# Cross-attention and a quantized feed-forward block on one core: another opening, and SyncE's transposes in another order

## The reference, cut to what matters

```python
x = x + xattn(layernorm(x), ctx)            # x: 4 x 2048 x 512, ctx: 4 x 154 x 512
x = x + ffn(layernorm(x), w1, b1, w2, b2, gamma, beta)

# xattn: the mask lets query i see key j only where j % 2048 == i
#   row i <  154:  out = (ctx[i] @ Wv) @ Wout + bout      (softmax of one term)
#   row i >= 154:  nothing is unmasked, all keys weigh the same:
#                  out = (mean(ctx) @ Wv) @ Wout + bout   (one row for the batch)
# ffn: h = layernorm(x)*gamma + beta
#   qlinear(h, w, b): round h to 8 bits by a scale per row, round w to -1, 0, 1
#     by the mean of |w| over the whole matrix, multiply, scale back, add b
#   out = qlinear(gelu(qlinear(h, w1, b1)), w2, b2)       # hidden 2048
```

## Time and profile before

| | |
|---|---|
| median of 3 runs (lowest, highest) | 584.91 us (582.09, 586.11) |
| profiled execution | 585.01 us, its span 583.3 us |
| mean granted TensorE clock | 0.965 |
| PE, DVE, ACT, POOL busy | 90%, 78%, 73%, 68% |

### The profile page before, as it was taken

One profiled execution on the slowest core, in us unless ns is written; L12 is line 12 of the kernel. 1 busy time (PEld: TensorE's weight loads), 2 busy tenths in 40 slices (PEclk: granted clock), 3 DMA queues, 4 the chain that ended last, 5 costly groups with the idle time before them and its releaser, 6 DMA issues.

```text
span 583.3 us, 7986 instructions
## 1 busy us (share of the span) xinstructions
PE 526.4 (90%) x2368; PEld 225.3 (39%) x2414; DVE 457.8 (78%) x754; ACT 424.5 (73%) x413; POOL 397.3 (68%) x530
## 2 busy tenths in 40 slices
PE   6968641798799998999999999999999999999997
PEld 3423210343344443444444444444444444444443
DVE  1167785986689897798998989898899989896553
ACT  0264443885688886888888888888888888887762
POOL 0016839886577878688887878787878787874100
PEclk9989775998999998999999999999999999999999
DMA  9992122455655556345555655555555555443432
GB/s 332 380 387 100 24 72 58 94 134 140 170 132 131 132 131 132 88 120 132 132 132 130 133 130 132 130 132 130 132 128 134 128 132 118 96 94 91 97 76 90
DMA packets 136686, 78.56 MB, mean 135 GB/s; under 512 B 114008, under 2 KB 114008, under 8 KB 136644
## 3 DMA queue, kind: packets, MB, share of 16 engines
q1 hardware_dynamic: 132948, 70.50, 48.4%
q10 hardware_dynamic: 3696, 7.55, 3.5%
HBM read 33.77 MB, written 17.00 MB: 87 GB/s over the span
## 4 chain that ended last, share of the span: by engine, by line
PE 66%; DMA 8%; POOL 7%; issue 6%; DVE 6%; SPq 3%; ACTq 3%; ACT 1%; POOLq 0%; DVEq 0%
PE py L841 31%; PE p L823 31%; DMA xqT<-xq 5%; PE p L816 3%; DMA hqT<-ctxm_d 3%; POOL hx L334 2%; SPq L219 2%; POOL xr L319 2%; DVE xr L681 1%; ACTq L454 1%; DVE stat L631 1%; POOL xr L338 1%; DVE w2q L622 1%; SPq L182 1%; POOL rstd L326 1%
## 5 line engine op out<-in xcount | busy, mean ns | idle before, releaser
L823 PE MATMUL p<-w1q,xqT 128*128 128x512 bf16 x996 | 237.2, 390 | 2.9 <-issue 2.0
L841 PE MATMUL py<-w2q,hqT 128*128 128x512 bf16 x1006 | 230.0, 379 | 1.0
L499 ACT ACTIVATE hid<-p,xdeq 128x1024 f32<-128x1024 f32 x128 | 141.9, 1110 | 40.0 <-PE p L823 39.8
L506 ACT ACTIVATE hq<-hid,hscale 128x2048 int8<-128x2048 f32 x64 | 128.1, 2002 | 45.6 <-DVE hscale L666 45.6
L841 PEld LDWEIGHTS py<-w2q,hqT 128*128 128x128 bf16 x1024 | 100.2, 98 | 120.8
L823 PEld LDWEIGHTS p<-w1q,xqT 128*128 128x128 bf16 x1024 | 97.1, 100 | 127.4 <-issue 26.6
L319 POOL TENSOR_TENSOR xr<-xr,attn 128x512 f32<-128x512 f32 (+1 forms) x61 | 86.5, 1438 | 13.3 <-issue 13.3
L660 DVE TENSOR_REDUCE hmax<-hid 128x1 f32<-128x1025 f32 x64 | 78.1, 1221 | 22.0 <-ACT hid L499 21.1
L656 DVE TENSOR_REDUCE hid<-hid 128x1 f32<-128x1024 f32 x64 | 77.5, 1211 | 18.7 <-ACT hid L499 18.7
L338 POOL TENSOR_TENSOR xr<-xr,b_b 128x512 f32<-128x512 f32 x64 | 87.3, 1384 | 0.0
L334 POOL TENSOR_TENSOR hx<-hx,beta_b 128x512 f32<-128x512 f32 (+1 forms) x63 | 80.6, 1300 | 1.7 <-ACT hx L486 1.7
(11 more groups left out here) (76 smaller groups left out, 284.7 us busy)
## 6 DMA issues: line engine op xcount, KB each, us to landing
out<-xr SPq DMA_DIRECT2D x64, 256.0 KB, 2.3
xr<-x SPq DMA_DIRECT2D x61, 256.0 KB, 3.0
wout<-wout_d ACTq DMA_DIRECT2D x8, 256.0 KB, 11.1
hid<-wvT SPq DMA_DIRECT2D x8, 256.0 KB, 12.2
raw<-w1T ACTq DMA_DIRECT2D x4, 512.0 KB, 11.6
raw<-w1T SPq DMA_DIRECT2D x4, 512.0 KB, 12.7
wout<-w2T SPq DMA_DIRECT2D x4, 512.0 KB, 8.2
xr<-w2T SPq DMA_DIRECT2D x2, 512.0 KB, 15.2
```

Of the source, the lines that this page charges most:

```text
L499: nc.scalar.activation(hid[:, t % 2, h * HALF:(h + 1) * HALF], p1[:, h * HALF:(h + 1) * HALF], ACT.Gelu, scale=col(xdeq, t)).then_inc(gelu ...
L506: nc.scalar.activation(hq8[:, t % 2, :], hid[:, t % 2, 0:HID], ACT.Copy, scale=col(hscale, t))\
L823: mm = nc.tensor.matmul(p1[:, n * D:(n + 1) * D], xT[:, k, :], w1q[:, k, n * D:(n + 1) * D], start=False, stop=(k == KD - 1))
L841: mm = nc.tensor.matmul(py[:, t % 2, :], hqT[:, t % 2, c // 2, c % 2, :], w2q[:, c, :], start=(c == 0), stop=(c == 2 * NJ - 1))
```

## The change

It does four things.

1. **Mean row of batch 0 from its own products.** Before, the row came out of Wv·Wout. Now the mean context row is made on PE first (two matmuls with ones, 128 and 26 rows), copied to all partitions by DVE; eight elementwise products of it with the Wv chunks (POOL for chunks 1, 2, 4, 6, 7, DVE for 0, 3, 5) are summed along the row by ACT (`mean_sum`), the sums weigh the Wout chunks on DVE (`mean_weighted`), and one matmul with ones, put after the 15th product, adds over partitions. The pick matrix is gone. The 108 rows are made much later, behind the first half of the first layer of tile 3.
2. **w2 in w1's raw buffer.** An eighth of w2 goes to `raw1` when w1 has been rounded there, so w2's loads wait for that rounding, and x tiles keep their own slots.
3. **Orders of the opening rewritten** on all five queues: Wv and Wout first, w1 behind them on SP alone, contexts later; x loads 0 to 13 before the loop; tiles 0 to 3 written out by hand; the loop starts at s = 4.
4. **In the loop** SP transposes the GELU bytes of tile s-1, then (odd s) the x pair, and only then stores and loads; POOL takes 1/std after the scale columns and adds b2 four tiles later.

```diff
+        w2raw = [raw1[:, j % 4, j // 4 * HALF:(j // 4 + 1) * HALF].rearrange("p (e n) -> p e n", e=2) for j in range(8)]
...
             def load_w2(j):
+                sp.wait_ge(wround_dve[0], j // 4 + 1)
+                sp.wait_ge(wround_act[0], j // 4 + 1)
...
             load_wv(0)
+            sp.dma_start(ctx_rows, ctx_b0[0:P, :]).then_inc(ctx_b0_loaded, 16)
+            sp.dma_start(ctx_end, ctx_b0[P:KV, :]).then_inc(ctx_b0_loaded, 16)
...
+            for s in range(4, T + LAG + 2):
+                if live(s - 1):
+                    transpose_h(s - 1)
+                if s % 2 == 1:
+                    for t in (s + 1, s + 2):
+                        if live(t):
+                            transpose_x(t)
                 if live(s - LAG - 1):
                     t = s - LAG - 1
                     sp.wait_ge(y_ready, t + 1)
                     sp.dma_start(out[t * P:(t + 1) * P, :], xr[:, t % XS, :]).then_inc(y_stored[t % XS], 16)
-                if live(s - 1):
-                    transpose_h(s - 1)
...
+            def mean_product(m):            # POOL; DVE has the same
+                pool.wait_ge(chunk_loaded[m], 32)
+                pool.wait_ge(ctx_mean_copied, 1)
+                if m >= 3:
+                    pool.wait_ge(vmean_done, m - 2)
+                pool.tensor_tensor(product[m % 3], wv[:, m // 4, m % 4, :], ctx_mean, ALU.mult).then_inc(vprod_pool, 1)
...
+            def mean_sum(m):                # ACT
+                nc.scalar.activation(product[m % 3], product[m % 3], ACT.Copy, accum_out=vmean[:, m:m + 1])\
+                    .then_inc(vmean_done, 1)
...
+            def mean_weighted(m):           # DVE
+                    nc.vector.scalar_tensor_tensor(mean_part, wout[:, m, :], vmean[:, m:m + 1], mean_part,
+                                                   ALU.mult, ALU.add).then_inc(mean_part_done, 1)
...
+            def weight_sum(j):
+                dve.wait_ge(wabs_dve[j], (3, 2)[j])
+                dve.wait_ge(wabs_act[j], (5, 6)[j])
...
+            context_mean()                  # PE
+            products(0, 15)
+            mean_row()
+            products(15, 31)
+            weight_total(0)
+            products(31, 32)
+            out_rows(0)
+            bias(0)
+            out_rows(1)
+            first_layer(0, 0)
+            first_layer(0, 1)
+            out_rows(2)
+            bias(1)
...
```

More of the change, by code:

```diff
@@ new lines, in _ @@
+            half_scale(0)
+            weight_sum(1)
+            hidden_scale(0)
+            weight_scale(1)
+            half_scale(1)
+            ctx_sum(2)
+            statistics(8)
+            x_scale(4, 2)
+            ctx_sum(3)
+            statistics(9)
+            round_weights(1, 0)
+            clip(1, 1)
+            hidden_scale(1)
+            ctx_means()
+            centre(7)
+            widen_h(0)
+            round_weights(1, 4)
+            clip(1, 2)
+            clip(1, 6)
@@ L752, in _ @@
+            clip(1, 7)
+            clip(1, 4)
+            clip(1, 0)
+            clip(1, 5)
+            tail_rows_out()
+            clip(1, 3)
+            half_scale(2)
+            centre(8)
+            attn_rows(1)
+            hidden_scale(2)
+            half_scale(3)
+            centre(9)
+            hidden_scale(3)
+            attn_rows(2)
+            attn_rows(3)
+            widen_h(1)
+            x_scale(6, 2)
+            for s in range(4, T + LAG + 1):
                 if live(s - 2):
@@ new lines, in first_layer @@
+            def first_layer(t, h):
+                xT = xqT[:, (t // 2) % 2, t % 2, :, :]
+                for n in (2 * h, 2 * h + 1):
+                    if t == 0:
+                        pe.wait_ge(wq_ready[0], n + 1)
+                    for k in range(KD):
+                        mm = nc.tensor.matmul(p1[:, n * D:(n + 1) * D], xT[:, k, :], w1q[:, k, n * D:(n + 1) * D],
+                                              start=False, stop=(k == KD - 1))
+                mm.then_inc(ffn1_done, 1)
@@ new lines, in second_layer @@
+            def second_layer(t):
+                pe.wait_ge(hcast_dve, t + 1)
+                pe.wait_ge(hcast_act, t + 1)
+                if t == 0:
+                    pe.wait_ge(tail_copied, 1)
+                    pe.wait_ge(wq_ready[1], 8)
+                elif t == 1:
+                    pe.wait_ge(attn_copied, B)
+                else:
+                    pe.wait_ge(y_ready, t - 1)
+                for c in range(2 * NJ):
+                    mm = nc.tensor.matmul(py[:, t % 2, :], hqT[:, t % 2, c // 2, c % 2, :], w2q[:, c, :],
+                                          start=(c == 0), stop=(c == 2 * NJ - 1))
+                mm.then_inc(ffn2_done, 1)
@@ L846 @@
+            bias(3)
+            first_layer(3, 0)
+            out_rows(3)
+            tail_product()
+            first_layer(3, 1)
+            second_layer(0)
+            for s in range(4, T + LAG):
+                if live(s):
+                    bias(s)
+                    first_layer(s, 0)
+                    first_layer(s, 1)
+                if live(s - LAG):
+                    second_layer(s - LAG)
 def kernel(x, ctx_1024, L0_xattn_Wq, L0_xattn_Wkv, L0_xattn_Wout, L0_xattn_bout,
```

570 lines of the change are left out of this document (313 added, 257 removed).

## The result

| | before | after |
|---|---|---|
| median (lowest to highest), 4 runs each | 585.51 us (582.09 to 586.2) | 556.32 us (554.85 to 556.81) |
| span of the profiled execution | 583.3 us | 554.9 us |
| mean granted TensorE clock | 0.965 | 0.988 |
| second layer of tile 0 starts | 111.17 us | 91.67 us |
| lost by PE after that start | 14.6 us | 5.7 us |

The ratio is 0.9508, 95% interval 0.9466 to 0.9551: 4.9% faster. 558 us was forecast, range 549 to 574. "Lost" is taken as in the frame of the sum: PE ends at 551.59, and 551.59 - 91.67 - 454.2 = 5.7. So 19.5 us come from the opening and 8.9 from the time after it, together the 28.4 by which the spans differ.

A forecast was written before the change was run, and what follows sets the result against it. PE was taken to bound the loop at 7.34 us a tile. Start 90, remaining work 454.2, lost 8, end 3.3 and profiled execution 1.7 gave 557.2, stated as 558 us, range 549 to 574.

The forecast's parts named there:

- frame of the sum: Once tile 0's second layer starts, PE still owes 454.2 us; the open questions are that start and the time lost after.
- The sum: Start 90, work 454.2, lost 8 and end 3.3 give a 555.5 us span; the profiled execution adds 1.7: 557.2.
- Part 1: Opening, mean row: ready inside the products, POOL's first add at 23 us instead of 47.20; products end near 37.5.
- Part 2: Opening, w1: loaded behind Wv and Wout with nothing lost; total at 36.7 us, rounded from 38.7 to 43.3.
- Part 3: Opening, w2's wait: loads start at 41.3 us, tile 0's x lands near 50, w2's scale is there at 69.
- Part 4: Opening from 66 us to tile 0's second layer: ACT is narrow, start at 90 us, bounds 86 and 98.
- Part 5: After the start: DVE comes late, odd-step x waits go; 8 us lost instead of 14.6, bounds 4 and 18.
- the loop's 6.6: Time after the start: the part of the gain still won if the opening's hole only moves, 6.6 us.
- rival D: Opening: the mean row did not hold tile 2, the hole moves, only the loop's 6.6 are won: 578 us; chance 0.05.
- B: Opening's chain is longer through late w2 and more ACT sums; start at 100 gives 568 us, 563 to 578; chance 0.20.
- E: Loop: SP blocks itself when x pairs are late, 4.75 us each; with 12 pairs 615 us; chance 0.07.
- C: Loop runs clean, DVE's lateness hides and the clock stays up, 2 us lost: 551 us; chance 0.06.

The follow-up runs named there:

- e1: The kernel before with SyncE's loop in the new order from step 4 on, nothing else: 572.95 us, ratio 0.9791.
- after_again: The changed kernel run once more, unedited, as yardstick of its group: 555.39 us, ratio 0.9491.
- e3: The changed kernel with POOL's even steps in the old order, 1/std ahead of the scale columns: 555.74 us, ratio 0.9494.
- e4: The changed kernel with POOL's first add made to wait until 31 of the 32 products are done: 569.8 us, ratio 0.9733.
- e5: The changed kernel with DVE's steps for b1's rows moved behind the mean row: 557.71 us, ratio 0.9538.
- e6: The changed kernel with the x transpose of tile 0 ahead of all w2 loads in SP's queue: 555.02 us, ratio 0.9471.
- v2: The changed kernel with e6, e7 and e9 together, and tile 1's transpose ahead of the loads of x tiles 12 and 13: 554.65 us, ratio 0.9472.
- e2: The changed kernel with SP's loop in the old order (store, bytes, load, spreads, x pair): 571.0 us, ratio 0.9753.
- e7: The changed kernel with DVE waiting for POOL's scale columns of tile 0 before rounding w1: 557.88 us, ratio 0.9533.
- e9: The changed kernel with the second out_rows on PE moved ahead of tile 0's bias product: 553.69 us, ratio 0.9467.
- e10: The changed kernel with SP's loop as bytes, store, load, spreads, x pair, so only the bytes precede the store: 573.52 us, ratio 0.9806.
- v3: v2 with DVE's last clip of w1 put ahead of the x scale of tile 2: 555.14 us, ratio 0.949.

## Why the prediction was right, and where it was not

The forecast's mechanism held, and 556.32 lies 1.7 us from 558, but this closeness is luck in part. Inside the opening two errors cancelled: the bias product of tile 1 came 7.6 us late, and the way from there to the start was 6.0 us shorter. Then the start was 1.7 us late and 2.3 us less were lost after it. The sum itself gives 557.2; the step from there to 558 has no reason behind it.

**The frame** held: the loop's step is 310.23 - 302.89 = 7.34 (second layer to second layer), and from PE's end to the end of the span it is 3.3. e1, where only 1.6 us are left over beside the 454.2, shows that 454.2 is close to what the work after the start costs.

**Part 1, the mean row.** POOL's first add came at 29.99 and not at 23, just past the bounds of 21 to 29. PE started at 5.92 instead of 4.38, its two context matmuls took 2.04 and 2.07 instead of 0.93 each, it waited 2.31 for the row's last step, and the row's matmul took 2.08. All three matmuls I had priced by the unbroken products of the earlier trace rows. The granted clock was 0.50 over the third of them, and in after_again and five others (e3, e4, e5, e6, v2) it took 1.12 or 1.13; it was 1.00 over the first two, which took double in every run, and why is left open. With this the products end at 44.7 instead of 37.5. The row's own chain was late too: POOL's products ended at 21.7 instead of 17.4, and DVE's three steps for b1's rows (19.3 to 23.0) stood ahead of its last steps. The step that a row at 21 to 29 is "still inside the products" was no guarantee that it costs nothing: e4 finds every microsecond of 11.9 more on the path. e5 finds no gain in 2.7 us less, but there w1's total was held up behind b1's rows.

**Part 2** had w1's total after its sums at 36.7; it came at 43.38, behind the products' delay, with DVE's sum ready only at 43.2.

**Part 3.** x of tile 0 landed at 57.39, not near 50. Of these 7.4 us some 6.5 come from w1's first rounding: w2's first load left at 47.75 instead of 41.3. The ring behind w2 had been priced right in kind: from w2's first load to the landing I had put near 9 us, and it took 9.6, the transpose itself 6.8 instead of 2.7. w2's scale was there at 74.31 instead of 69.

**Part 4** named 90 for the start, and 91.67 and 90.04 came. But from the bias of tile 1 to the start I had counted 62.4 to 90, 27.6 us, and nine runs show 21.65: 70.01 to 91.67 after, 68.40 to 90.04 in after_again, and as much in e2, e3, e4, e5, e7, e9 and e10. Where PE met more holes on the way it was 22.1 (v2), 23.3 (e6) and 24.3 (v3). Here is the step that failed: the "first layer at low clock 5.3" of tile 0 I had also put on tiles 1 and 2, and 2.5 and up to 2.6 on the halves of tile 3. They took 3.63, 3.4 to 3.6, 1.90 and 1.89, which with the bias products is some 5 of the 6 us; the last one is the microsecond that I had added for small waits. PE is nearly unbroken there, at a granted clock of 0.98 where the earlier trace rows showed 0.73 and 0.68. Those low values came with the old holes, and I carried them over to a stretch that no longer had any. That three engines meet at the start held: PE's last half layer ended at 91.63, DVE's last clip of w2 at 91.5, ACT's widening of tile 0 at 91.1.

**Part 5.** Lost time came out at 5.7 instead of 8, with the two waits I had named (2.23 for DVE's late widening, forecast 2; 1.39 for x of tile 6, forecast up to 3.7) and one slow layer, 1.7 us. The mis-sized term is "the loop's 6.6" of rival D, which is 14.6 - 8. The 8 held some 7 us that the new opening costs the loop, so 6.6 is not what SP's order is worth: with the opening as it was, the order won 12.9 (e1, 1.6 lost instead of 14.6), and on the new opening 15.6 (e2 lost 20.4). And of the two reasons I gave, "ahead of a store that waits for DVE and of three spreads", the store's wait is not needed: e10 has the x pair behind a store that waited for nothing, only behind the issue of store, load and spreads, and loses as much as e2. How the loss is shared among those three was not tried. In the step at 111 us of e2 the later landing (2.9 us) counts for more than the later issue (1.9).

**The rivals.** B (the opening's chain is longer) was true up to 70 us, and the faster run from there made up for it; the start was nowhere near its 100. D falls by the time itself (its 578 against 556) and by e4. E (a late x pair blocks SP) left no trace: after 120 us PE lost nothing but issue. C's clean loop was nearly there in e1, 1.6 us lost.

## What to carry to other kernels

Before a part is credited only with the waits it removes from the old profile, ask what the other parts of the change would lose without it: on the new opening the old transpose order cost 15.6 us and on the old one 12.9, though these 2.7 us are little more than the runs' own spread. In the loop the transposes went ahead of the plain loads and broadcasts of their queue, and that counted twice, at their issue and at their landing; in the opening the same move (e6) only passed the wait on to the next tile. Do not carry a low granted clock from a stretch with holes over to the same work without them. Independent matmuls can go into the hole that is left (e9), since this needs no other engine's slack, but what it wins is not shown beyond the runs' spread.

## What the runs showed of the hardware

- Transposes of the x of one tile land in 2.6 to 2.7 us alone, 5.2 to 5.5 behind an x tile's load and the three spreads, 6.8 behind half of w2 and 9.0 behind all of it and two x tiles (e10, e2, after, e6).
- POOL and DVE slow each other both ways while DVE rounds or clips w1: POOL's copy 0.29 against 3.04 us, a one-column operation 0.19 against 1.29, DVE's rounding 1.28 against 2.28 (after, e7). DVE's row sums (L702) beside POOL's adds cost neither: two adds took 2.49 us as alone.
- A layer after a wait of over 2 us took 4.9 to 5.3 us instead of 3.6 in many cases, at a granted clock of 0.68 to 0.73, so that the wait cost some 1.3 to 1.7 us beyond its length. But not always: after a wait of 2.2 us for DVE the same layer took some 5.3 in seven runs and 3.63, at a granted clock of 1.00, in four (e2, e6, e7, v2), and after one of 3.17 us for x it took 3.63 in e3.
- The first two context matmuls took 2.04 and 2.07 us at a granted clock of 1.00, against 0.93 for each of the unbroken products; the third took 2.08 at 0.50 in the changed kernel and 1.12 at 1.00 in e3.
